# Rounding the transposed rows on ScalarE instead of VectorE in an attention and mixture-of-experts block

## The chip, the cores and the metric

The kernel runs on one core of one Trainium2 chip. The metric is device time in microseconds (us) of one execution. Three timed runs of the kernel before gave 1981.57, 1982.76 and 1986.39 us; the median is 1982.76 us. A further execution was recorded by the hardware profiler and took 1988.57 us, of which the trace covers a span of 1986.8 us.

The engines are named as in the trace: PE is TensorE (PEld its weight loads), ACT is ScalarE, DVE is VectorE, POOL is GpSimd, SP is SyncE, which issues most of the transfers.

## The reference

The input is 4 batches of 2048 rows of 512 floats. One block computes, cut to what matters here:

```
h = layernorm(x) * (1 + ca) + sa
x = x + ga * attention(h)            # segments of 128 rows, plus a global term
h = layernorm(x) * (1 + cb) + sb
x = x + gb * experts(h)              # 16 experts, top 1, capacity 512, D=512, H=2048
```

`sa, ca, ga, sb, cb, gb` are rows of 512 numbers for each batch, computed from a condition vector. The attention has `softmax(Q K^T / sqrt(32))` over 128 rows of a segment, all 512 features at once. The router takes the largest of 16 logits of every row.

## The kernel before

**Precision.** PE multiplies in a reduced float32 form (`fp32r`). To keep float32 accuracy, each operand `a` is split into `a_hi` (rounded to that form) and `a_lo = a - a_hi`, and each product is made of three matmuls (`split3`, lines 322 to 324): hi*hi, hi*lo, lo*hi.

**Stage 1, attention and router, until about 730 us.** The 8192 rows are worked off in 16 groups of 512 rows; `iteration(i)` of every engine works on group `i` and, in a software pipeline, on parts of groups `i-1`, `i-2` and `i-3`, and at its end prepares group `i+1`. The order on each engine is written out by hand, and semaphores tie the engines together. The folded weights `m` (query times key) and `v` (value times output) are split once before the loop. For the normalised, transposed rows of group `i+1` the steps at the end of an iteration are:

- PE, `transpose_xn`, line 602: 16 transposes of `xa` into the four PSUM banks `big[0..3]`, one bank for each chunk `k` of 128 features.
- ACT, `modulate`, line 957: for each `k` one activation `bank * (1 + ca) + sa` into `ht[:, k, :]`, an SBUF tile of 128x512 float32; both `(1 + ca)` and `sa` are 128x1 operands.
- DVE, `split_rows`, lines 1219 and 1221: for each `k` a copy `ht -> ht_hi` that rounds to fp32r (a CAST in the trace), then, after a wait for that copy, `ht_lo = ht - ht_hi`, and the semaphore `ht_split`.
- PE, `g_tile(i+1, 0)`: 12 matmuls into `big[0]`; before each chunk `k` it waits for `ht_split` of that chunk. `g_tile(i+1, 1)` to `(i+1, 3)` use the same rows again. `ht` itself is read once more by the score product (line 774), `ht_hi` and `ht_lo` by the `u` product with `v`.

After `g_tile 0` and `g_tile 1` PE transposes the second-norm rows `h2` of group `i-2` (line 706), ACT rounds them to `h2t_hi` (line 1032) and DVE makes `h2t_lo` (line 1368) for the router logits. DVE then goes through a long list: the statistics of the next rows (1150), softmax remainders, ranks of the router, `h` and `xr` (1387, 1391) from the attention output, statistics again, `u_lo` (1409) and the query constants (1275). PE may reuse a bank for the transposes of `xa` only when `u_lo` has been taken from it.

Meanwhile POOL scales and shifts the second-norm rows of group `i-1` in SBUF: four pairs of a multiply (line 1621) and an add (line 1625), each 128x512. PE's line 706 of the next iteration waits for all of them (`h2_ready`).

**Stage 2, the experts, from about 760 us.** For each of 16 experts rows are gathered by indirect DMA, and two layers of `split3` products run over weights that are loaded and split on the way. None of the lines of the change is used in it.

Of the kernel before, what the change touches and what calls it, by code (L numbers as in the profile page):

```python
# [30 lines left out]
ACT = mybir.ActivationFunctionType  # L31
# [29 lines left out]
def build_block(nc, x, wq, bq, wk, bk, wv, bv, wo, bo, wg, bg, w1, b1, w2, b2, cond, wmod, out):  # L61
# [39 lines left out]
    def keep(name, shape, dt):  # L101

        t, end = at(name, shape, dt, cursor[0])
        cursor[0] = end + (-end) % 32
        return t
# [7 lines left out]
    def over(start, *tensors):  # L113

        made = []
        for name, shape, dt in tensors:
            t, start = at(name, shape, dt, start)
            made.append(t)
        return made
# [12 lines left out]
    mod_col = keep("mod_col", [P, 2, KC, NBATCH], F32)  # L132
# [37 lines left out]
    ht = over(r_ht, ("ht0", full, F32), ("ht1", full, F32))  # L170
    ht_hi, ht_lo = over(r_split, ("ht_hi", full, F32R), ("ht_lo", full, F32R))
# [69 lines left out]
    def sem(name):  # L241
        return stack.enter_context(nc.semaphore(name))
# [23 lines left out]
    xr_in = [sem(f"xr_in{i}") for i in range(2)]  # L266
    grows_in = [sem(f"grows_in{i}") for i in range(2)]
    ln1_step, ln1_ready, ln1_rstd, xn_done = (sem(k) for k in ("ln1_step", "ln1_ready", "ln1_rstd", "xn_done"))
    t1_full, ht_full, ht_hi_done, ht_split, qc_raw, qc_ready = (sem(k) for k in (
        "t1_full", "ht_full", "ht_hi_done", "ht_split", "qc_raw", "qc_ready"))  # L270
    gt_full, gt_done, u_full, u_hi_done, u_split = (sem(k) for k in (
        "gt_full", "gt_done", "u_full", "u_hi_done", "u_split"))
    s_full, mx_step, negb_ready, exp_done, prec_ready, prob_ready = (sem(k) for k in (
# [43 lines left out]
    def batch_of(g):  # L317
        return g.n // GPB
# [13 lines left out]
    def pro_bank(q):  # L332
        return banks[q % 8 if q < MODS[GA] else 4 + q % 4]
# [586 lines left out]
    def _(act):  # L920
# [31 lines left out]
        def modulate(g):  # L952

            for k in range(KC):
                act.wait_ge(t1_full, 4 * g.n + k + 1)
                act.wait_ge(pro_evac, MCOL + 1)
                act.activation(ht[g.par][:, k, :], big[k][:, :], ACT.Identity,
                               bias=mod_col[:, 0, k, bass.ds(batch_of(g), 1)],
                               scale=mod_col[:, 1, k, bass.ds(batch_of(g), 1)]).then_inc(ht_full, 1)

        def add_u(g, j):

            act.wait_ge(gt_full, 4 * g.n + j + 1)
            act.activation(gt[:, j, :], big[j][:, :], ACT.Identity, bias=u_col[:, j:j + 1]).then_inc(gt_done, 1)

        modulate(Group(0, 0))
        modulation_row(GA)
        act.wait_ge(pro_full, HGT + 1)
        for k in range(KC):
            for b in range(NBATCH):  # L970
                seg = slice(b * (NSEG // NBATCH), (b + 1) * (NSEG // NBATCH))
                ins = act.activation(hg_t[:, k, seg], pro_bank(HGT)[:, k * NSEG + seg.start:k * NSEG + seg.stop],
                                     ACT.Identity, bias=mod_col[:, 0, k, b:b + 1], scale=mod_col[:, 1, k, b:b + 1])
# [6 lines left out]
        for k in range(KC):  # L980
            ins = act.activation(gg_t[:, k, :], pro_bank(GGT)[:, k * NSEG:(k + 1) * NSEG], ACT.Identity,
                                 bias=u_col[:, k:k + 1])
# [16 lines left out]
        def iteration(i, cur, prev, prev2, nxt, prev3):  # L999
# [57 lines left out]
            if nxt:  # L1057
                modulate(i.plus(1))
# [67 lines left out]
    def _(dve):  # L1126
# [88 lines left out]
        def split_rows(g):  # L1215

            for k in range(KC):
                dve.wait_ge(ht_full, 4 * g.n + k + 1)
                dve.tensor_copy(ht_hi[:, k, :], ht[g.par][:, k, :]).then_inc(ht_hi_done, 1)  # L1219
                dve.wait_ge(ht_hi_done, 4 * g.n + k + 1)  # L1220
                dve.tensor_tensor(ht_lo[:, k, :], ht[g.par][:, k, :], ht_hi[:, k, :].bitcast(F32), ALU.subtract) \  # L1221
                    .then_inc(ht_split, 1)

        split_rows(Group(0, 0))

        dve.wait_ge(gsum_xn, 1)
# [117 lines left out]
        def iteration(i, cur, prev, prev2, nxt, prev3):  # L1344
# [66 lines left out]
            if nxt:  # L1411
                split_rows(i.plus(1))
# [308 lines left out]
```

## Time and profile before

| quantity | value |
|---|---|
| median of three runs | 1982.76 us |
| profiled execution | 1988.57 us, span of the trace 1986.8 us |
| PE busy | 1866.8 us (94%), 9137 matmuls |
| DVE busy | 1315.1 us (66%), 2006 instructions |
| ACT busy | 780.6 us (39%), 1257 instructions |
| POOL busy | 863.5 us (43%), 709 instructions |
| mean granted clock of PE | 0.972 of full speed |

The shares are averages over two stages. From 194.0 to 686.0 us, which is twelve iterations of stage 1, PE is busy for 454.0 us, DVE for 445.7 us, POOL for 258.8 us and ACT for 183.9 us of 492 us, so DVE, not much of a bound over the whole span, is nearly as full as PE there.

A busy time in the trace includes the time in which an instruction has started and cannot yet proceed, for example because a memory port is held by another engine. So one line can have several durations.

### The profile page before, as it was taken

Reading aid. Unit: us, or ns where it says so; the run is one execution under the profiler, and the core shown is the slowest. Engines: PE = TensorE matmul, PEld = TensorE weight load, DVE = VectorE, ACT = ScalarE, POOL = GpSimd, SP = SyncE. Lnnn points to the kernel's source line nnn. Section 1 sums busy time; section 2 is a strip of 40 time slices with the busy share of each in tenths; the row PEclk is TensorE's granted clock in tenths of the full one; section 3 lists DMA queues with packets and bytes.
Section 4 is the critical chain, followed back from the end, with each engine's and each line's share of the span. In section 5 each row is a group of like instructions: output and inputs, shape, how many; then the busy total and the mean of one; then the engine's idle time right before and its main releaser. Section 6 shows DMA issues by size and latency. Waiting matters only on the chain.

```text
span 1986.8 us, 28205 instructions
## 1 busy us (share of the span) xinstructions
PE 1866.8 (94%) x9137; PEld 1517.2 (76%) x9138; DVE 1315.1 (66%) x2006; ACT 780.6 (39%) x1257; POOL 863.5 (43%) x709
## 2 busy tenths in 40 slices
PE   8998999989998973999999999999899999999998
PEld 3476777767777752788888888888888888888886
DVE  4378899998999875445655555354756878454763
ACT  2333333333343421333443433334535655333541
POOL 2034455644555443134434334233655766342632
PEclk9999999999999985999999999999999999999999
DMA  7143222332224342344354434434554556434531
GB/s 259 32 144 134 86 86 85 124 130 85 85 86 154 100 149 68 103 170 151 121 182 141 163 133 135 161 116 162 190 174 143 202 178 220 139 131 166 190 110 64
DMA packets 137916, 270.77 MB, mean 136 GB/s; under 512 B 17634, under 2 KB 18222, under 8 KB 137863
## 3 DMA queue, kind: packets, MB, share of 16 engines
q1 hardware_dynamic: 115338, 221.27, 31.8%
q0 software_dynamic: 22528, 48.86, 7.5%
q8 instruction: 29, 0.48, 0.1%
q14 instruction: 21, 0.16, 0.0%
HBM read 237.71 MB, written 50.72 MB: 145 GB/s over the span
## 4 chain that ended last, share of the span: by engine, by line
PE 70%; DVE 20%; issue 6%; ACT 2%; POOL 1%; DMA 1%; DVEq 0%; POOLq 0%; ACTq 0%; SPq 0%
PE bank L322 21%; PE bank L323 21%; PE bank L324 21%; DVE stats L1150 3%; DVE ht_hi L1219 3%; DVE ht_lo L1221 2%; DVE prob L1275 2%; DVE h L1387 2%; DVE xr L1391 2%; DVE u_lo L1409 1%; DVE h2t_lo L1368 1%; PE bank L817 1%; PE bank L563 1%; PE bank L531 1%; PE bank L591 1%
## 5 line engine op out<-in xcount | busy, mean ns | idle before, releaser
L1448 DVE TENSOR_TENSOR h_lo<-h_f,h_hi 128x512 fp32r<-128x512 f32 x256 | 221.0, 884 | 368.2 <-ACT h_f L1088 368.1
L1087 ACT ACTIVATE h_hi<-bank,b_col 128x512 fp32r<-128x512 f32 x256 | 176.4, 689 | 601.7 <-PE bank L324 589.9
L322 PE MATMUL bank<-bt_hi,w_hi 128*128 128x512 f32 (+4 forms) x1024 | 361.4, 353 | 7.8 <-DVE w_lo L1419 5.6
L323 PE MATMUL bank<-bt_lo,w_hi 128*128 128x512 f32 (+4 forms) x1024 | 360.3, 352 | 0.0
L324 PE MATMUL bank<-bt_hi,w_lo 128*128 128x512 f32 (+4 forms) x1024 | 360.2, 352 | 0.0
L322 PE MATMUL bank<-w_hi,h_hi 128*128 128x512 f32 x832 | 327.3, 393 | 3.8 <-DVE h_lo L1448 2.6
L323 PE MATMUL bank<-w_lo,h_hi 128*128 128x512 f32 x832 | 325.4, 391 | 0.0
L324 PE MATMUL bank<-w_hi,h_lo 128*128 128x512 f32 x832 | 325.1, 391 | 0.0
L322 PEld LDWEIGHTS bank<-bt_hi,w_hi 128*128 128x128 f32 x1024 | 195.4, 191 | 33.2 <-issue 9.0
L323 PEld LDWEIGHTS bank<-bt_lo,w_hi 128*128 128x128 f32 x1024 | 195.2, 191 | 21.1
L324 PEld LDWEIGHTS bank<-bt_hi,w_lo 128*128 128x128 f32 x1024 | 195.1, 191 | 20.4
L1644 POOL DMA_INDIRECT gb_rows<-mod_rows,tok_g x64 | 78.0, 1219 | 279.2 <-DVE tok_g L1525 221.7
L322 PEld LDWEIGHTS bank<-w_hi,h_hi 128*128 128x128 f32 x832 | 157.0, 189 | 36.9 <-issue 5.6
L324 PEld LDWEIGHTS bank<-w_hi,h_lo 128*128 128x128 f32 x832 | 156.9, 189 | 33.1
L323 PEld LDWEIGHTS bank<-w_lo,h_hi 128*128 128x128 f32 x832 | 157.1, 189 | 31.1
L1440 DVE TENSOR_TENSOR w_lo<-raw,w_hi 128x2048 fp32r<-128x2048 f32 x64 | 151.6, 2369 | 40.4 <-ACT w_hi L1077 40.4
L1644 POOL DMA_INDIRECT xh<-h_rows,tok_h x64 | 89.3, 1396 | 201.6 <-DVE tok_h L1507 178.2
L1088 ACT ACTIVATE h_f<-bank,b_col 128x512 f32<-128x512 f32 x256 | 174.3, 681 | 0.0
L1568 POOL TENSOR_TENSOR per_tok<-per_tok,half_neg 128x4 f32<-128x4 f32 (+1 forms) x33 | 33.4, 1013 | 279.7 <-DVE per_tok L1157 279.7
L1419 DVE TENSOR_TENSOR w_lo<-raw,w_hi 128x2048 fp32r<-128x2048 f32 x64 | 151.5, 2368 | 2.2
L322 PE MATMUL bank<-ht_hi,m_hi 128*128 128x512 f32 x256 | 113.6, 444 | 33.6 <-DVE ht_lo L1221 31.0
L1670 POOL TENSOR_TENSOR yo<-yo,gb_rows 128x512 f32<-128x512 f32 x60 | 98.5, 1642 | 106.4 <-DVE yo L1469 105.0
(256 smaller groups left out, 3375.1 us busy)
## 6 DMA issues: line engine op xcount, KB each, us to landing
raw<-in_L_ffn_W_dram SPq DMA_DIRECT2D x128, 1024.0 KB, 5.5
xa<-in_L_attn_x_dram SPq DMA_DIRECT2D x16, 1024.0 KB, 5.4
xr<-in_L_attn_x_dram SPq DMA_DIRECT2D x16, 1024.0 KB, 8.0
out_dram<-xr SPq DMA_DIRECT2D x16, 1024.0 KB, 9.9
h_rows<-h SPq DMA_DIRECT2D x16, 1024.0 KB, 4.6
b_bc<-in_L_ffn_b_dram SPq DMA_DIRECT2D x16, 256.0 KB, 6.3
wm_b<-in_L_wmod_dram SPq DMA_DIRECT2D x2, 1024.0 KB, 8.3
wm_d<-in_L_wmod_dram SPq DMA_DIRECT2D x2, 1024.0 KB, 5.1
```

What stands on the lines that cost most here:

```text
L322: pe.matmul(o, a_hi, b_hi, start=start, stop=False)
L323: pe.matmul(o, a_hi, b_lo, start=False, stop=False)
L324: return pe.matmul(o, a_lo, b_hi, start=False, stop=stop)
L1087: act.activation(h1_hi[b % 2][:, j, :], h_bank[j][:, :], ACT.Relu, bias=bias)
L1088: act.activation(h1_f[:, j, :], h_bank[j][:, :], ACT.Relu, bias=bias).then_inc(relu_done, 1)
L1150: dve.bn_stats(st[0:parts, s, :], rows[:, s, :]).then_inc(step, 1)
L1219: dve.tensor_copy(ht_hi[:, k, :], ht[g.par][:, k, :]).then_inc(ht_hi_done, 1)
L1419: dve.tensor_tensor(w1_lo[b % 2][:], raw[2 * (b % 2)][:], w1_hi[b % 2][:].bitcast(F32), ALU.subtract) \
L1440: dve.tensor_tensor(w2_lo[b % 2][:], raw[2 * (b % 2) + 1][:], w2_hi[b % 2][:].bitcast(F32), ALU.subtract) \
L1448: dve.tensor_tensor(h1_lo[b % 2][:, j, :], h1_f[:, j, :], h1_hi[b % 2][:, j, :].bitcast(F32), ALU.subtract) \
L1644: pool.indirect_dma_start(out=rows[:, j, :], out_offset=None, in_=source, in_offset=bass.IndirectOffsetOnAxis(tokens[:, j:j + 1], 0), boun ...
L1670: pool.tensor_tensor(yo[:, j, :], yo[:, j, :], gb_rows[:, j, :], ALU.mult).then_inc(y_scaled, 1)
```

## The change

ACT writes the rounded half itself. For each chunk it runs the same activation from the same PSUM bank twice, first into `ht_hi` (fp32r), then into `ht` (float32), and the semaphore `ht_full` is raised by the second. DVE's copy, and its wait for that copy, are gone; DVE only subtracts. The other splits of the kernel stay as they are.

```diff
-                act.activation(ht[g.par][:, k, :], big[k][:, :], ACT.Identity,
-                               bias=mod_col[:, 0, k, bass.ds(batch_of(g), 1)],
-                               scale=mod_col[:, 1, k, bass.ds(batch_of(g), 1)]).then_inc(ht_full, 1)
+                for rows in (ht_hi, ht[g.par]):
+                    ins = act.activation(rows[:, k, :], big[k][:, :], ACT.Identity,
+                                         bias=mod_col[:, 0, k, bass.ds(batch_of(g), 1)],
+                                         scale=mod_col[:, 1, k, bass.ds(batch_of(g), 1)])
+                ins.then_inc(ht_full, 1)
...
             for k in range(KC):
                 dve.wait_ge(ht_full, 4 * g.n + k + 1)
-                dve.tensor_copy(ht_hi[:, k, :], ht[g.par][:, k, :]).then_inc(ht_hi_done, 1)
-                dve.wait_ge(ht_hi_done, 4 * g.n + k + 1)
                 dve.tensor_tensor(ht_lo[:, k, :], ht[g.par][:, k, :], ht_hi[:, k, :].bitcast(F32), ALU.subtract) \
                     .then_inc(ht_split, 1)
```

On ACT, the end of the iteration of group 2 before (`logit_parts` are the router's partial logits, `ht_102` the rows of group 3, `prob` the softmax of the next iteration):

```order
L1014 ACTIVATE h_1_111<-xr_106,per_tok 128x512 x3
L1007 ACTIVATE u_hi<-bank 128x512
L1014 ACTIVATE h_1_111<-xr_106,per_tok 128x512
L1011 ACTIVATE logit_parts<-bank 32x512
L957 ACTIVATE ht_102<-bank,mod_col 128x512 x4
L1020 ACTIVATE prob,per_tok<-bank,per_tok 128x128 x4
```

and the same place in the changed kernel:

```order
L1016 ACTIVATE h_1_111<-xr_106,per_tok 128x512 x3
L1009 ACTIVATE u_hi<-bank 128x512
L1016 ACTIVATE h_1_111<-xr_106,per_tok 128x512
L1013 ACTIVATE logit_parts<-bank 32x512
L958 ACTIVATE ht_hi<-bank,mod_col 128x512
L958 ACTIVATE ht_102<-bank,mod_col 128x512
L958 ACTIVATE ht_hi<-bank,mod_col 128x512
L958 ACTIVATE ht_102<-bank,mod_col 128x512
L958 ACTIVATE ht_hi<-bank,mod_col 128x512
L958 ACTIVATE ht_102<-bank,mod_col 128x512
L958 ACTIVATE ht_hi<-bank,mod_col 128x512
L958 ACTIVATE ht_102<-bank,mod_col 128x512
```

Four activations have become eight; what stands before them and behind them is the same.

On DVE, the end of an iteration before (`ht_101` are the next group's rows):

```order
L1275 SCALAR_TENSOR_TENSOR prob,per_tok<-xa_100,vc_tab 128x512 x4
L1279 TENSOR_SCALAR per_tok<-per_tok,qc_bc 128x4
L1409 TENSOR_TENSOR u_lo<-bank,u_hi 128x512 x2
L1219 CAST ht_hi<-ht_101 128x512
L1221 TENSOR_TENSOR ht_lo<-ht_101,ht_hi 128x512
L1219 CAST ht_hi<-ht_101 128x512
L1221 TENSOR_TENSOR ht_lo<-ht_101,ht_hi 128x512
```

and the same place in the changed kernel:

```order
L1275 SCALAR_TENSOR_TENSOR prob,per_tok<-xa_100,vc_tab 128x512 x4
L1279 TENSOR_SCALAR per_tok<-per_tok,qc_bc 128x4
L1409 TENSOR_TENSOR u_lo<-bank,u_hi 128x512 x2
L1221 TENSOR_TENSOR ht_lo<-ht_101,ht_hi 128x512 x4
L1350 TENSOR_REDUCE per_tok<-bank 128x4
```

The pair of CAST and subtraction, which stood there four times, is one subtraction four times. PE, POOL and SP have the same rows as before.

## Rows read from the trace of the kernel before

**Rows 1.** Part 4 of the page: shares of the chain that ended last.

```profile
PE 70%; DVE 20%; issue 6%; ACT 2%; POOL 1%; DMA 1%; DVEq 0%; POOLq 0%; ACTq 0%; SPq 0%
```

**Rows 2.** Waits from 100 to 740 us: who waited for whom, us, times, longest.

```profile
PE bank L322 <- DVE ht_lo L1221: 31.0, 15, 2.2
...
PE bank L602 <- DVE u_lo L1409: 9.0, 12, 1.0
```

**Rows 3.** Timeline of PE, 437 to 446 us: start, duration, instruction, idle before.

```profile
437.86 0.39 PE L323 MATMUL bank<-ht_lo,m_hi 128*128 128x512 f32 x1
438.09 0.40 PE L324 MATMUL bank<-ht_hi,m_lo 128*128 128x512 f32 x1
440.57 0.50 PE L322 MATMUL bank<-ht_hi,m_hi 128*128 128x512 f32 x1 [2.08 <-DVE ht_lo L1221]
...
441.63 0.51 PE L322 MATMUL bank<-ht_hi,m_hi 128*128 128x512 f32 x1
441.98 0.39 PE L323 MATMUL bank<-ht_lo,m_hi 128*128 128x512 f32 x1
...
445.15 1.91 PE L706 MATMUL bank<-ident,h 128*128 128x128 f32 x16
```

**Rows 4.** Timeline of DVE, 432 to 449 us.

```profile
432.17 0.41 DVE L1219 CAST ht_hi<-ht 128x512 fp32r<-128x512 f32 x1
432.61 1.64 DVE L1221 TENSOR_TENSOR ht_lo<-ht,ht_hi 128x512 fp32r<-128x512 f32 x1
434.18 1.49 DVE L1219 CAST ht_hi<-ht 128x512 fp32r<-128x512 f32 x1
...
437.30 1.51 DVE L1219 CAST ht_hi<-ht 128x512 fp32r<-128x512 f32 x1
438.84 1.67 DVE L1221 TENSOR_TENSOR ht_lo<-ht,ht_hi 128x512 fp32r<-128x512 f32 x1
440.44 0.41 DVE L1219 CAST ht_hi<-ht 128x512 fp32r<-128x512 f32 x1
440.88 0.69 DVE L1221 TENSOR_TENSOR ht_lo<-ht,ht_hi 128x512 fp32r<-128x512 f32 x1
...
446.56 2.48 DVE L1368 TENSOR_TENSOR h2t_lo<-bank,h2t_hi 128x512 fp32r<-128x512 f32 x4 [1.50 <-ACT h2t_hi L1032]
```

**Rows 5.** Timeline of POOL, 430 to 440 us.

```profile
430.99 1.27 POOL L1621 TENSOR_TENSOR h<-h,cb_tab 128x512 f32<-128x512 f32 x1
432.44 1.27 POOL L1625 TENSOR_TENSOR h<-h,sb_tab 128x512 f32<-128x512 f32 x1 [0.18 <-POOL h L1621]
433.67 1.71 POOL L1621 TENSOR_TENSOR h<-h,cb_tab 128x512 f32<-128x512 f32 x1
435.56 1.27 POOL L1625 TENSOR_TENSOR h<-h,sb_tab 128x512 f32<-128x512 f32 x1 [0.18 <-POOL h L1621]
...
438.71 1.26 POOL L1625 TENSOR_TENSOR h<-h,sb_tab 128x512 f32<-128x512 f32 x1 [0.18 <-POOL h L1621]
```

**Rows 6.** Timeline of ACT, 430 to 434 us.

```profile
430.65 1.45 ACT L957 ACTIVATE ht<-bank,mod_col 128x512 f32<-128x512 f32 x2
```

**Rows 7.** Part 5 of the page, and lines by form: activations into either type.

```profile
L1087 ACT ACTIVATE h_hi<-bank,b_col 128x512 fp32r<-128x512 f32 x256 | 176.4, 689 | 601.7 <-PE bank L324 589.9
...
L957 ACT ACTIVATE ht<-bank,mod_col 128x512 f32<-128x512 f32 x64 | 46.1, 772 | 7.5 <-PE bank L602 7.0
```

**Rows 8.** Windows: length, busy PE, PEld, DVE, ACT, POOL, granted clock, DMA, GB/s.

```profile
153.00:194.00 41.00, 37.98 (x193) 29.94 (x193) 32.38 (x61) 15.04 (x30) 18.46 (x17) 0.96 0.30 103
...
440.60:480.40 39.80, 36.87 (x198) 28.98 (x198) 36.71 (x81) 15.43 (x31) 21.47 (x20) 1.00 0.30 105
...
482.00:484.00 2.00, 2.00 (x6) 1.59 (x5) 1.75 (x9) 1.60 (x10) 0.00 (x0) 0.50 0.85 324
...
644.40:686.00 41.60, 38.40 (x197) 30.03 (x197) 37.08 (x81) 15.19 (x31) 21.69 (x20) 0.96 0.24 81
```

**Rows 9.** Timeline of DVE at 116 us, in the first iteration.

```profile
116.36 0.69 DVE L1350 TENSOR_REDUCE per_tok<-bank 128x4 f32<-128x512 f32 x1 [1.02 <-PE bank L774]
```

More of the change, by code:

```diff
@@ L268, in build_block @@
     ln1_step, ln1_ready, ln1_rstd, xn_done = (sem(k) for k in ("ln1_step", "ln1_ready", "ln1_rstd", "xn_done"))
-    t1_full, ht_full, ht_hi_done, ht_split, qc_raw, qc_ready = (sem(k) for k in (
-        "t1_full", "ht_full", "ht_hi_done", "ht_split", "qc_raw", "qc_ready"))
+    t1_full, ht_full, ht_split, qc_raw, qc_ready = (sem(k) for k in (
+        "t1_full", "ht_full", "ht_split", "qc_raw", "qc_ready"))
     gt_full, gt_done, u_full, u_hi_done, u_split = (sem(k) for k in (
```

## The prediction

> **What bounds the kernel now.** I read the chain that ended last first: PE is most of it, but DVE has a fifth [rows 1], which is about 400 us, and DVE's lines in it (ht_hi, ht_lo, stats, h, xr, u_lo) belong to stage 1. So stage 1 is bound by PE and DVE in turn, and the list of waits says where they hand over: PE stood still 15 times, 31.0 us in all, for ht_lo, which comes from the routine that is changed, and 9.0 us in 12 waits of at most 1.0 us for u_lo [rows 2]. The next view is one steady iteration in time. PE has the first two chunks of g_tile 0 and then stops until 440.57, idle for 2.08 us; chunk 3 follows late at 441.63 [rows 3]. DVE at that time is inside split_rows, from 432.17 to 441.57, without a gap [rows 4].
>
> Why this takes 9.4 us for eight instructions is the thing to see. A CAST takes 0.41 us alone and 1.49 to 1.51 us in the middle, a subtraction 0.69 us alone and 1.64 to 1.67 us in the middle [rows 4]. The long ones end just after an instruction of POOL: POOL's add of 432.44 ends at 433.71 and DVE's subtraction at 434.25; POOL's multiply of 433.67 ends at 435.38 and DVE's CAST at 435.67 [rows 4, 5]. And that multiply takes 1.71 us instead of 1.27. The two engines take turns: whichever comes second stands until the other's instruction is through. When POOL is done, at 439.97, DVE is back at 0.41 and 0.69 us. The Trainium skill (SBUF — State Buffer, section "Who interferes with whom") says that VectorE copies, and subtractions with two SBUF inputs, share a port pair with GpSimd under an exclusive lock; the trace agrees with its 1.64 us against 0.69 us.
>
> The last view is the granted clock by windows of one iteration each. Of thirteen windows from 153 to 686 us, eight read 0.96 and five 1.00; the first, one at 1.00 and the last stand in [rows 8]. In each of the eight the clock is at its lower level, 1.2 GHz, only for a short stretch right behind the stall, as in the 2 us from 482 us, which read 0.50 [rows 8]; nowhere else in these iterations did it fall. A ninth such stretch follows the last stall, at 686 us.
>
> **The change part by part.** There are 16 calls of split_rows; one is in the prologue, one in the first iteration, and the other 14 are the crossings between iterations that show this stall.
>
> ACT, added: four more activations a group. Two of the old kind take 1.45 us back to back, so 0.725 us each [rows 6]. An activation that writes fp32r is not slower than one that writes float32 as far as rows show (0.689 us for h_hi with one column operand, 0.772 us for ht with two [rows 7]); bounds 0.689 and 0.772 us, less some overlap, I take 0.725. ACT begins at 430.65 [rows 6]; the pairs end at 432.1, 433.6, 435.0 and 436.5. Before, the first was there at 431.4. Nothing else is queued on ACT until the exponentials, which wait for DVE's maximum after 441.5; 2.9 us of more work lie in an idle stretch.
>
> DVE, removed: four CASTs, 0.41 + 1.49 + 1.51 + 0.41 = 3.8 us of its time, with what they waited for POOL in them. What is left is four subtractions which still meet POOL. I lay them out by the turns just read: after POOL ends, DVE is through in 0.54 us (433.71 to 434.25), and POOL's next one has started 0.13 us before that [rows 4, 5]. DVE is free at 432.17 and the first pair of ACT is there at 432.1; POOL's multiply ends at 432.26 and its add can only start at 432.44, so the first subtraction fits in front of it and ends near 432.9. Add 432.7 to 434.0; second subtraction to 434.5; multiply to 435.7; third (rows there at 435.0) to 436.2; add to 437.3; fourth (rows there at 436.5) to 437.9. So ht_lo is complete near 437.9 instead of 441.6, 3.7 us earlier.
>
> PE, the gain: chunk 2 would be wanted at 438.09 + 0.23 = 438.32 and chunk 3 at 439.0. Both subtractions are done by then, with 1.1 us to spare at chunk 3. Matmuls follow each other at 0.23 us (437.86 to 438.09). The stops cost 440.57 - 438.32 = 2.25 us; the three matmuls of chunk 2 then last until 441.63, 1.06 us instead of 0.69, since chunk 3 is late too; and the first step of chunk 3 is 0.35 us instead of 0.23 [rows 3]. Together 2.7 us a crossing, 0.6 of it above the idle time of 2.08. Over all: 31.0 us of idle time [rows 2] and 14 crossings of a little over 0.5 us, 7 us; 38 us.
>
> The clock: a window at 0.96 of 41.5 us has lost 0.04 * 41.5 = 1.7 us. Nine of these make 15 us. I expect them to go with the stall, because they only stand behind it, while the shorter stops for u_lo have none behind them. Bounds: 0 and 15 us; I take 15, by the row at 0.50 that lies behind a stop.
>
> What is late next: DVE's h2t_lo follows PE's line 706 by 1.41 us (446.56 after 445.15, DVE idle 1.50 before) [rows 3, 4]. PE reaches 706 2.7 us earlier, DVE is ready for it 3.7 us earlier, so DVE's idle time there grows to about 2.5 us and it stays tied to PE. From h2t_lo to u_lo DVE's list is unchanged, and it sets PE's wait for u_lo at line 602, 9.0 us over 12 iterations [rows 2], as before. That wait remains, since both of its ends move along with line 706. So the iteration becomes its old length less the stall: 39.8 - 2.7 = 37.1 us where the clock had held.
>
> POOL: its eight instructions end near 440.4 instead of 439.97, since the first subtraction now goes in front of an add. PE's line 706 of the next iteration, which waits for them, comes at 442.4 instead of 445.15. The cover shrinks from 5.2 us to 2.0 us; it holds. SP's transfers follow the same events and none of PE's waits in [rows 2] is for one, so I cost them at nothing.
>
> Where the change costs: in the first iteration POOL is not there, and CAST and subtraction took DVE 0.41 and 0.69 us as in the last pair of [rows 4], faster than ACT's pair of 1.45. Over four chunks that is 4 * (1.45 - 1.10) = 1.4 us later, but DVE idled 1.02 us there for PE's scores anyway [rows 9]; 0.5 us. The prologue is covered by PE's other products. I book 1 us for both, and 1 us for stops of PE at chunk 3 that I do not see.
>
> Sum: 38 + 15 - 2 = 51 us. The profiled execution took 1988.57 us (span 1986.8), so 1937.6 us by it. That execution stands 5.8 us above the median of the runs, 1982.76; against the median the forecast is 1932 us. Stage 2 is unchanged.
>
> **Rivals.**
>
> The clock keeps falling. Its low stretches may come from the thin work before the stall (transposes, the small score matmuls) and not from the stall itself. For it: five of the stalls of the same 2.08 us had no low stretch behind them, so the stall alone does not decide. Against it: all nine sit behind a stall, none elsewhere in the steady part. Then only the 38 - 2 = 36 us are gained: 1947 us.
>
> DVE loses a turn. If a subtraction arrives just after POOL has started, it stands for the whole of POOL's instruction. The first one has 0.2 us of margin at 432.26 to 432.44; if it misses, everything behind it moves by a turn of 1.67 us, the fourth ends near 439.6 and PE stops 0.7 us at chunk 3. If two are missed, PE stops 1.5 us or more; with 1.2 us won in a crossing and half of the clock it is 14 * 1.2 + 7 = 24 us, 1959 us. Of the skill's page the sentence "Issue order, not op shape, decides who blocks" says the same: who comes first decides; by it the order above holds only while ACT's pairs come in time.
>
> Slower: ACT's pair becomes the pace. If the activation into fp32r from this form cost so much that eight of them last beyond 441.6 - 0.7 - 430.65 = 10.2 us, that is above 1.28 us each, ht_lo would be later than now. At 1.4 us each PE would stop 1 us longer in each of 14 crossings: 1983 + 14 = 1997 us. The rows have nothing above 0.772 us for an activation of this size [rows 7], so this is remote.
>
> No gain: DVE's list is the true bound, and PE's lead is given back at line 602 as a longer wait for u_lo. Then 1981 us. Against it: DVE is idle 1.5 us before h2t_lo in the steady iteration, so DVE isn't what closes the loop, and it gets more idle there.
>
> **How the numbers follow.** Forecast 0.70, its own range 1924 to 1941. Clock stays 0.12 (1947). A turn or two lost 0.12 (1940 to 1962). No gain 0.03, slower 0.03. The range for 8 in 10 reaches from 1924, where the waits for u_lo also shrink by some 8 us, to 1956. A difference below 0.3%, 6 us, can't be told from none. Faster 0.94, same 0.03, slower 0.03.
>
> **What would show it.** In the profile after: the wait of line 322 for ht_lo gone or below 0.7 us in the steady iterations; the subtraction still at 1.1 to 1.7 us for most of them, so the port is still shared; ACT's pair at 1.45 us; DVE's idle time before h2t_lo up from 1.5 to about 2.5 us; the granted clock at 1.00 in the iteration windows; the iteration at 37 to 38 us; nothing moved behind 760 us but the start. The prediction is wrong if line 322 still waits 2 us, if line 706 waits for POOL, or if the wait at line 602 grows by what was saved.

## The result, and the profile after

Four runs of the changed kernel gave 1928.79 to 1933.73 us, median 1930.35 us; before it was 1984.58 us with one more run taken beside them. The ratio is 0.9727, 95% interval 0.9702 to 0.9752: 54 us faster, where 51 were forecast and 1932 us predicted. In a second set of runs the ratio was 0.9714 (0.9701 to 0.9727). The span of the trace went from 1986.8 to 1927.1 us, 59.7 us less; the profiled execution of the kernel before took 4 us more than its median, so the traces differ by more than the medians. Stage 2 (first matmul of the experts to the end) lasts 1198.9 us before and 1196.1 after, so all but 2.8 us of the 59.7 come in stage 1. One of the eight runs of the kernel before that stand beside the last two experiments took 6274.66 us; it is left out of their ratios.

The waits from 100 to 720 us in the changed kernel, as who waited for whom, us in total, times, longest; they answer to [rows 2]:

```profile
DVE ht_lo L1221 <- ACT ht L958: 19.3, 33, 2.3
...
PE bank L602 <- DVE u_lo L1409: 8.5, 12, 0.9
...
PE bank L322 <- DVE ht_lo L1221: 1.0, 2, 0.7
```

PE's 31.0 us in 15 waits for ht_lo are 1.0 us in 2, both at chunk 3, in the first two crossings (at 148.51 and 185.16 us). Its wait for u_lo stayed (9.0, now 8.5). The wait that is new is DVE's for ACT: the subtraction is bound by ACT's pace in places, and but for that 1.0 us PE comes later still and loses nothing by it.

PE from 406 us, one steady iteration, to be read against [rows 3] (start, duration, instruction):

```profile
406.03 0.48 PE L322 MATMUL bank<-ht_hi,m_hi 128*128 128x512 f32 x1
...
407.27 0.39 PE L324 MATMUL bank<-ht_hi,m_lo 128*128 128x512 f32 x1
407.50 0.39 PE L322 MATMUL bank<-ht_hi,m_hi 128*128 128x512 f32 x1
...
408.18 0.39 PE L322 MATMUL bank<-ht_hi,m_hi 128*128 128x512 f32 x1
...
411.58 1.91 PE L706 MATMUL bank<-ident,h 128*128 128x128 f32 x16
```

All 24 matmuls of g_tile 0 and 1 follow each other at about 0.23 us. From the first of them to line 706 it is 5.55 us; before it was 445.15 - 436.84 = 8.31 us, 2.76 more.

DVE in the same iteration, against [rows 4]; `x2` are two instructions in one row:

```profile
401.40 0.69 DVE L1221 TENSOR_TENSOR ht_lo<-ht,ht_hi 128x512 fp32r<-128x512 f32 x1
402.74 1.03 DVE L1221 TENSOR_TENSOR ht_lo<-ht,ht_hi 128x512 fp32r<-128x512 f32 x1 [0.64 <-ACT ht L958]
404.08 3.05 DVE L1221 TENSOR_TENSOR ht_lo<-ht,ht_hi 128x512 fp32r<-128x512 f32 x2 [0.31 <-ACT ht L958]
407.05 0.68 DVE L1350 TENSOR_REDUCE per_tok<-bank 128x4 f32<-128x512 f32 x1
407.77 0.53 DVE L1353 SCALAR_TENSOR_TENSOR per_tok<-per_tok 128x4 f32<-128x4 f32 x1
...
412.99 2.48 DVE L1368 TENSOR_TENSOR h2t_lo<-bank,h2t_hi 128x512 fp32r<-128x512 f32 x4 [1.56 <-ACT h2t_hi L1034]
```

The first subtraction is alone (0.69 us), the others take turns with POOL. From the first one's start to the last one's end it is 5.7 us, before with the CASTs 9.4 us.

ACT there, against [rows 6]:

```profile
399.92 0.78 ACT L958 ACTIVATE ht_hi<-bank,mod_col 128x512 fp32r<-128x512 f32 x1
400.60 0.77 ACT L958 ACTIVATE ht<-bank,mod_col 128x512 f32<-128x512 f32 x1
401.26 0.78 ACT L958 ACTIVATE ht_hi<-bank,mod_col 128x512 fp32r<-128x512 f32 x1
...
404.58 0.81 ACT L958 ACTIVATE ht<-bank,mod_col 128x512 f32<-128x512 f32 x1
```

And POOL, against [rows 5]:

```profile
400.18 1.27 POOL L1621 TENSOR_TENSOR h<-h,cb_tab 128x512 f32<-128x512 f32 x1
401.63 1.59 POOL L1625 TENSOR_TENSOR h<-h,sb_tab 128x512 f32<-128x512 f32 x1 [0.18 <-POOL h L1621]
...
406.54 1.74 POOL L1621 TENSOR_TENSOR h<-h,cb_tab 128x512 f32<-128x512 f32 x1
408.46 1.30 POOL L1625 TENSOR_TENSOR h<-h,sb_tab 128x512 f32<-128x512 f32 x1 [0.18 <-POOL h L1621]
```

ACT's pair comes every 1.33 us. POOL's add of 401.63 is longer (1.59 instead of 1.27): the first subtraction went in front of it. POOL ends at 409.76, 1.8 us before line 706 asks for its rows.

The granted clock in windows of 37 us, one that holds the crossing whose stall was the first with a low clock behind it before, and a later one (columns as in [rows 8]):

```profile
148.00:185.00 37.00, 36.12 (x192) 28.83 (x192) 29.23 (x56) 17.71 (x34) 20.28 (x18) 1.00 0.36 127
...
371.00:408.00 37.00, 36.12 (x198) 29.00 (x197) 32.98 (x77) 17.89 (x35) 21.95 (x21) 1.00 0.34 112
```

Every window from 111 to 631 us reads 1.00. An iteration lasts 37.15 us (line 602 at 215.05 and, eleven iterations later, at 623.68), where it had been 41.0 us on average (stalls at 193.98 and, twelve later, at 686.03). Fourteen crossings at 3.85 us are 54 us.

### The profile page after: what moved, and what is told of

It reads as the page before. It is cut to its first block, busy times and chain, and to the rows that moved or that the text cites. A ratio compares the mean times of both kernels' runs of the same rounds, so it can differ in the third digit from the quotient of the medians.

```text
span 1927.1 us, 28205 instructions
## 1 busy us (share of the span) xinstructions
PE 1839.8 (95%) x9137; PEld 1504.4 (78%) x9138; DVE 1258.2 (65%) x1942; ACT 822.6 (43%) x1321; POOL 871.1 (45%) x709
## 4 chain that ended last, share of the span: by engine, by line
PE 75%; DVE 16%; issue 5%; ACT 2%; POOL 1%; DMA 1%; DVEq 0%; POOLq 0%; ACTq 0%; SPq 0%
PE bank L322 22%; PE bank L324 22%; PE bank L323 22%; DVE stats L1152 3%; PE bank L774 3%; DVE prob L1275 2%; DVE h L1387 2%; DVE xr L1391 2%; DVE h2t_lo L1368 1%; PE bank L817 1%; PE bank L563 1%; DVE u_lo L1409 1%; PE bank L602 1%; PE bank L531 1%; PE bank L591 1%
## 5 line engine op out<-in xcount | busy, mean ns | idle before, releaser
L1079 ACT ACTIVATE w_hi<-raw 128x2048 fp32r<-128x2048 f32 x64 | 122.6, 1916 | 0.0
```

The source lines that it names most:

```text
L1079: act.activation(w2_hi[b % 2][:], raw[2 * (b % 2) + 1][:], ACT.Copy).then_inc(w2_hi_done, 1)
```

## The experiments

All are compared with the kernel before on the same chip. First, is it GpSimd that makes the CAST dear? Two kernels cut POOL's multiply and add of the second-norm rows to 4 of 512 columns, one of the kernel before and one of the changed kernel.

```diff
-                    rows = h2[p1.par][:, s, :]
+                    rows = h2[p1.par][:, s, 0:4]
...
-                    pool.tensor_tensor(rows, rows, cb_tab[:, bass.ds(b, 1), :].rearrange("p b d -> p (b d)"), ALU.mult) \
+                    pool.tensor_tensor(rows, rows, cb_tab[:, bass.ds(b, 1), 0:4].rearrange("p b d -> p (b d)"), ALU.mult) \
```

> The kernel before, but GpSimd's multiply and add of the second-norm rows (lines 1621 and 1625) touch only 4 of 512 columns, so the rows are left unscaled but for these. Theory A (VectorE's CAST and subtraction cost 3.8 us a group because they take turns with GpSimd): without these eight instructions the CAST takes 0.41 us and the subtraction 0.69 us every time, split_rows takes 4.4 us instead of 9.4, TensorE's stall for ht_lo and the low clock behind it go, and the time falls from 1984 to 1920 to 1932 us without any change of split_rows. Rival B (the time of the CAST is its own, GpSimd's overlap is a coincidence): CAST stays at 1.5 us in the middle pairs, the stall stays at 2.1 us, time 1980 to 1988 us.

Measured: 1912.59 us, ratio 0.9636 (0.9622 to 0.9651). Lines by form, 194 to 660 us, columns as in [rows 7]:

```profile
L1221 DVE TENSOR_TENSOR ht_lo<-ht,ht_hi 128x512 fp32r<-128x512 f32 x48 | 33.2, 692 | 1.6
L1219 DVE CAST ht_hi<-ht 128x512 fp32r<-128x512 f32 x48 | 20.2, 421 | 13.4 <-ACT ht L957 13.4
```

> The changed kernel with the same cut of GpSimd's multiply and add to 4 columns. Theory A: with no turns to take, the removed CAST is worth nothing more; the time equals that of the kernel before with the same cut, within 4 us, near 1920 us (0.8 us a group less than the changed kernel, since the query constants lose their turn too and u_lo is no longer late). Rival B: the gain of the change is independent of GpSimd, so this kernel is still some 50 us faster than the kernel before with the same cut.

Measured: 1910.73 us, ratio 0.9628 (0.9613 to 0.9643).

Rival B fell in both. With POOL's overlap gone the CAST takes 0.421 us and the subtraction 0.692 us each time, PE has no wait for ht_lo left, and the change is then worth 2 us instead of 54, which the intervals can't tell from none. Both times missed what I expected: the first is 7 us below the range, the second 9 us below 1920. Seen from line 706 to line 706 an iteration lasts 36.05 us in the second kernel, 1.1 us less than in the changed one where I had counted 0.8, and the last two, in which the loop runs out, are 3.3 and 0.8 us shorter; PE's wait of 3.1 us for POOL's last add is gone there. From its first expert matmul on, the first kernel takes the same 1196.1 us as the changed one, so none of the miss is in stage 2.

Second, each side of the change alone. ScalarE does its pair, and VectorE still copies:

```diff
+                for rows in (ht_hi, ht[g.par]):
+                    ins = act.activation(rows[:, k, :], big[k][:, :], ACT.Identity,
...
                 dve.tensor_copy(ht_hi[:, k, :], ht[g.par][:, k, :]).then_inc(ht_hi_done, 1)
```

> One part alone: ScalarE writes both halves as in the change, and VectorE still does its CAST into ht_hi. Theory A: ScalarE's four more activations lie in its idle time and the first chunk is ready no later than VectorE is; the same as before within 3 us (1982 to 1988). Rival C (the added work costs, and is hidden under a larger gain of the removal): 5 to 15 us slower than before, with TensorE's stall for ht_lo at 2.5 us or more.

Measured: 1983.35 us, ratio 0.9996 (0.9986 to 1.0007). With the CASTs in place the added work costs nothing that can be measured, so the gain comes with their removal. PE's wait, 100 to 720 us, is that of [rows 2] again:

```profile
PE bank L322 <- DVE ht_lo L1223: 31.7, 16, 2.2
```

Third, the clock. The stall is kept, and PE is given something to do in it:

```diff
             for k in range(KC):
+                if k == 2:
+                    for _ in range(filler):
+                        pe.matmul(lg_bank[:, :], m_hi[:, 0, chunk(0)], v_hi[:, 0, :], start=True, stop=True)
...
-                g_tile(i, 0)
+                g_tile(i, 0, 8 if prev2 else 0)
```

> The kernel before with eight more matmuls of 512 columns (0.23 us each, 1.8 us, into a bank that nothing reads then) in g_tile 0 ahead of chunk 2, that is inside the 2.1 us stall. Theory A (the low clock comes of the stall): the stall is still there in time, but TensorE is busy in it, the granted clock stays at 1.00 in the iteration windows, and the time falls by the clock's share of the forecast, some 15 us, to 1965 to 1973 us. Rival D (the low clock comes of the thin work around it): the clock still reads 0.96 in about eight windows and the time stays at 1984 us.

Measured: 1971.33 us, ratio 0.9933 (0.9918 to 0.9948), that is 13 us less for 8 more matmuls an iteration. The window from 194 to 640 us of this kernel, columns as in [rows 8]:

```profile
194.00:640.00 446.00, 430.17 (x2281) 337.69 (x2281) 410.56 (x883) 171.52 (x347) 237.61 (x220) 1.00 0.31 106
```

The same window of the kernel before:

```profile
194.00:640.00 446.00, 413.25 (x2154) 323.60 (x2155) 404.24 (x878) 168.66 (x341) 233.47 (x218) 0.98 0.29 100
```

Rival D fell: the transposes and the small products around the stall are the same, and the clock holds once PE is busy in it. Behind the eight matmuls PE still waits, 0.3 us in a steady crossing, so they don't make it later.

Fourth, how much room ScalarE has. The added activations go, inside the loop, to tiles that VectorE overwrites:

```diff
-                for rows in (ht_hi, ht[g.par]):
+                for rows in (*extra, ht_hi, ht[g.par]):
...
-                modulate(i.plus(1))
+                modulate(i.plus(1), (ht_lo,))
```

and in the second kernel `(ht_lo, h2t_lo)`.

> The changed kernel with a third activation for each chunk inside the loop, into ht_lo, where VectorE overwrites it. Each chunk then comes every 2.0 us (3 * 0.665) instead of 1.33. Theory A: rows of chunk 3 are ready 2.65 us later than in the changed kernel, at 7.98 + 0.1 us after ScalarE's start; TensorE wants the last ht_lo 8.3 us after that start, so it is late by 0.5 to 1.5 us with the turns: 0.5 to 1.5 us an iteration, 7 to 20 us slower than the changed kernel (1937 to 1951), and the clock stays high since the stall is short. Rival F (ScalarE's pair has room for a third activation): within 3 us of the changed kernel.

Measured: 1945.89 us, ratio 0.9801 (0.9786 to 0.9816); 17 us slower than the changed kernel beside it (1928.53), in the upper part of what theory A gave. Rival F fell.

> The changed kernel with four activations for each chunk, the added ones into ht_lo and h2t_lo, which VectorE overwrites. Chunks come every 2.66 us, the last after 10.6 us, ht_lo 11.4 us or more after ScalarE's start, when TensorE wants it at 8.3: theory A gives 3 us or more an iteration, 42 to 50 us, plus a low clock behind each longer stall (up to 25 us more where every iteration has one): 1975 to 2005 us, at or above the kernel before. This is the slower rival of the prediction put to the test, at 4 * 0.665 = 2.66 us a chunk. Rival F: TensorE's other waits absorb part of it, 1945 to 1970 us.

Measured: 2003.86 us, ratio 1.0096 (1.0079 to 1.0112), slower than the kernel before and at the upper end of theory A. PE's wait from 194 to 640 us with three activations:

```profile
PE bank L322 <- DVE ht_lo L1221: 6.8, 13, 0.7
```

and with four:

```profile
PE bank L322 <- DVE ht_lo L1221: 30.5, 21, 2.1
```

The windows over the same stretch read a clock of 1.00 with three and 0.96 with four: the stops of 0.5 to 0.7 us have no low stretch behind them there, while with four activations (stops of 1.9 to 2.2 us, most with a second one of 0.7 to 1.1 us close by) ten of the 14 crossings do. In its first iteration the kernel with three has one too, behind a stop of 0.68 and one of 1.04 us (0.50 from 120 to 122 us). The slower rival is a real mechanism: ScalarE's pace begins to cost between two and three activations a chunk, and between three and four the kernel falls behind the kernel before.

Last, the wait that is left, for u_lo. VectorE's list is reordered: one segment of the query constants stands before u_lo of bank 2, two before bank 3 and one behind it, where all four had stood before bank 2. The changed kernel runs beside it as reference.

> The changed kernel itself beside the others of this set, as their reference on the same chip: 1928 to 1934 us, ratio 0.972 to 0.975 to the kernel before. A gain that depends on the chip would show as a ratio outside of this.

Measured: 1928.53 us, ratio 0.9714 (0.9701 to 0.9727), a little below the 0.972 that I expected at least; the interval covers it. The edit of the next kernel:

```diff
-                    if s == 2:
-                        query_const(i)
+                    if s >= 2:
+                        query_const(i, (0,) if s == 2 else (1, 2))
                     dve.wait_ge(u_hi_done, 4 * n + s + 1)
...
+                query_const(i, (3,))
```

> The changed kernel with VectorE's order at the end of an iteration changed: the query constants (line 1275) of segment 0 stand before u_lo of bank 2, those of segments 1 and 2 before u_lo of bank 3, that of segment 3 and the closing line 1279 behind it, so that bank 3 is free about 1.7 us sooner. Theory A (TensorE's remaining wait at line 602, 0.63 to 0.89 us in most iterations, is VectorE's list being late with u_lo): the wait goes and 6 to 9 us with it, 1921 to 1925 us. Rival E (the wait is given back at once as a stall for ht_lo, since the subtractions start later against TensorE): a new stall of up to 0.8 us, time within 2 us of the changed kernel.

Measured: 1923.56 us, ratio 0.9688 (0.9675 to 0.9702), 5.0 us better than the changed kernel beside it (theory A had 6 to 9) and the fastest kernel here that leaves nothing out; the intervals of the two ratios touch, but the runs themselves do not overlap (1920.95 to 1925.25 against 1927.39 to 1929.11). Both theories had a part: the 8.5 us for u_lo are gone but for 0.3, and some came back as a wait for ht_lo (100 to 720 us):

```profile
PE bank L322 <- DVE ht_lo L1221: 4.9, 12, 0.7
```

I read this as the turns again: the query constants of line 1275 have both inputs in SBUF, and now two of the four meet POOL instead of one (1.83 and 1.16 us in the iteration at 394 us), so they take 1.07 us on average instead of 0.93.

I then moved the last segment behind split_rows:

```diff
-                query_const(i, (3,))
             if nxt:
                 split_rows(i.plus(1))
+            if cur:
+                query_const(i, (3,))
```

> As the reordered query constants on top of the change, but the last segment and the closing line 1279 stand behind split_rows. VectorE is then free for the subtractions some 2 us sooner and does the last segment in the 1.5 us that it idles before h2t_lo. Theory A: the 4.9 us that came back as waits for ht_lo go as well, 1917 to 1921 us. Rival G: the last segment, now between split_rows and the maximum of the scores, delays the exponentials and h2t_lo by about 1 us, which TensorE then waits for: 1923 to 1930 us.

Measured: 1957.54 us, ratio 0.9858 (0.9841 to 0.9874): theory A fell, and rival G had named the right place but far too small a price. Waits from 194 to 640 us:

```profile
PE bank L706 <- ACT gt L966: 15.2, 12, 1.6
DVE h2t_lo L1369 <- ACT h2t_hi L1034: 10.3, 12, 0.9
PE bank L322 <- DVE h2t_lo L1369: 5.3, 12, 0.4
```

The chain goes over three engines. The segment and line 1279 meet POOL and last 2.8 us; the maximum, and ACT's exponentials that wait for it, start later; and ACT's emptying of `gt` stands in its queue behind the exponentials, so PE can't reuse banks 0 and 1 for line 706. I had looked at DVE's idle time before h2t_lo and not at what ACT has queued behind the exponentials. Nor were the subtractions sooner by 2 us: DVE now waits 1.80 us for ACT before the first of them (at 415.91 us). And the clock fell again. Of the ten stops of 1.1 to 1.6 us for `gt`, each followed by one of 0.4 to 0.6 us for h2t_lo, six have a low stretch behind them; the four stops of 0.6 to 0.7 us have none. One of the six:

```profile
427.83 1.24 PE L706 MATMUL bank<-ident,h 128*128 128x128 f32 x8 [1.50 <-ACT gt L966]
429.62 0.66 PE L322 MATMUL bank<-ht_hi,m_hi 128*128 128x512 f32 x1 [0.44 <-DVE h2t_lo L1369]
...
430.00:432.00 2.00, 2.00 (x6) 1.56 (x5) 2.00 (x5) 0.30 (x1) 0.00 (x0) 0.50 0.94 318
```

> The kernel before with the query constants reordered as in the first of these kernels and nothing else. Theory A (in the kernel before, the last thing that PE waits for in an iteration is ht_lo, and that is set by VectorE's own list, not by when PE gets bank 3): the wait for u_lo at line 602 goes, the stall for ht_lo grows by as much, and the time stays within 4 us of the kernel before. Rival H (waits of PE add up, each can be taken away on its own): 5 to 9 us faster, as it was on top of the change.

Measured: 2001.65 us, ratio 1.0088 (1.0073 to 1.0103), 17 us slower. Both theories missed it. PE's stalls in one iteration:

```profile
400.65 0.51 PE L322 MATMUL bank<-ht_hi,m_hi 128*128 128x512 f32 x1 [1.25 <-DVE ht_lo L1221]
...
403.77 0.79 PE L322 MATMUL bank<-ht_hi,m_hi 128*128 128x512 f32 x1 [2.15 <-DVE ht_lo L1221]
```

The window from 194 to 640 us:

```profile
194.00:640.00 446.00, 409.48 (x2068) 322.05 (x2080) 396.15 (x854) 159.77 (x330) 228.12 (x210) 0.94 0.28 99
```

Theory A had the direction: the wait at line 602 is gone and the wait for ht_lo took its place. But it is larger than the one it replaced (3.4 us against 2.1 + 0.8). Two of the query segments now meet POOL instead of one, and DVE's list from its first u_lo to the first CAST lasts 7.7 us instead of 7.3. The clock is lower for it (0.94 against 0.98), with a low stretch in every crossing. Rival H fell. The same edit gains 5 us on one kernel and costs 17 us on the other; I read that as what the change did: in the kernel before DVE's list decides when an iteration ends, in the changed one it no longer does.

## Why the prediction was right

- **What bounds the kernel.** Right. The turns with POOL make the price of the CAST (the cut of POOL's work took it away), and the stall for ht_lo is where most of it reaches PE. The waits for u_lo (9.0 us) went with POOL's work as well, so they hang on the turns too.
- **ScalarE's pair costs nothing.** Right, by the kernel that has only this part: 0.9996. I had 1.45 us for a pair; it is 1.33 us, since the step between activations back to back is 0.66 to 0.67 us and I had spread the whole time of two.
- **The turns of the four subtractions.** Right: 5.7 us laid out, 5.7 us in the trace. The one margin that I had called thin, the first subtraction in POOL's gap, held in each iteration from 215 us on (0.68 or 0.69 us). In the second crossing it took 1.15 us, and there PE stopped for 0.28 us.
- **The stall.** 38 us forecast, somewhat too low. The filler kernel splits the gain: 13 us belong to the clock, so 41 us are left for the stall and what hangs on it. What I had not booked is a second stop. I took 39.8 us as the length of an iteration in which the clock holds, but some such iterations last 40.6 or 40.7 us, with a stop of 0.4 us for line 1387 (`h`) in the middle and a later u_lo:

```profile
416.95 0.50 PE L322 MATMUL bank<-v_hi,ht_hi 128*128 128x512 f32 x1 [0.40 <-DVE h L1387]
```

  PE has five of these (1.9 us; some 0.9 us each with what follows, so about 4 us, an estimate) in the kernel before. The kernels that still have the CASTs all have five, with POOL's work cut too; the kernels without the CASTs have none. Why the change takes them away stays open.
- **The clock.** 15 us forecast, 13 us by the filler kernel, and all windows of the loop at 1.00 after. The nine low stretches were those of the one execution that was profiled, 1988.57 us, 4 us above the median. The kernel with only ScalarE's pair, which has the same stall, shows six, and took 1980.97 us; so 15 us was near by some luck, and the share of the clock differs between executions.
- **What is late next.** Half right. h2t_lo follows line 706 by 1.41 us as before, and the waits for u_lo stayed. But DVE's idle time there is 1.56 us and not 2.5: POOL now ends later against DVE's list, so small instructions behind split_rows meet it (line 1353, 0.53 us instead of 0.16; line 1297, 0.67 instead of 0.22). 0.8 of the 0.9 us went into these two. Nothing hung on it.
- **Where it costs.** The 1 us booked for stops at chunk 3 came: 1.0 us in two waits, in the first crossings. The 1 us for the first iteration and the prologue was not needed; PE has no wait for ht_lo there. The first iteration has a difference between the traces that is not the change's. Its 16 transposes took 3.59 us at a low clock before and 1.97 after:

```profile
109.12 3.59 PE L602 MATMUL bank<-ident,xa 128*128 128x128 f32 x16 [1.96 <-POOL xa L1578]
```

  They take 1.96 or 1.97 us in all ten other kernels' traces too, the filler kernel's and that with only ScalarE's pair among them, and in the changed kernel's second trace. So the 1.6 us belong to that one execution of the kernel before. The idle 1.02 us of DVE [rows 9], on which I counted, came of the same low clock.
- **The sum.** 51 us against 54 of the medians. Between the two traces, to which its terms belong, it is 59.7 us: besides what was booked, some 4 us of the stops for `h`, 1.6 us of the transposes and 2.8 us of stage 2. The first is the part of the change that I missed. The other two belong to the execution: stage 2, 1198.9 us in the trace before, lasts 1194.9 to 1197.3 us in the eleven others, with the CASTs and without.
- **The rivals.** The clock rival fell to the filler kernel. A lost turn was not seen in the steady iterations. The slower rival, put at 1.28 us or more for an activation, was brought about with four activations a chunk, that is 1.33 us for each of the old two, and gave 2004 us, more than the 1997 us that I had for 1.4 us: I had left out that the stops make the clock fall.

## What to carry to other kernels

Where two engines take turns, the price of an instruction is what it waits for, not what it computes: the CAST of 0.42 us cost 1.5 us in the middle, twice a group. Moving it to ScalarE, whose activation takes 0.78 us with POOL's work and with that work cut, was worth 54 us, and the second activation cost nothing. Before you take an engine's idle time for room, follow what its neighbours have queued behind the event you delay; 1.5 us of idle time in DVE was not room for one segment. And a wait that is not the last in its iteration can't be taken away alone: the same reordering gained 5 us after the change and lost 17 before it.

## What was not expected of the hardware

The stall of 2.1 us in each crossing cost PE some 13 us through the clock, beside the 41 us of the stall and what hung on it; eight useless matmuls in it made the kernel 13 us faster. Not every stall had a low stretch behind it: nine of 14 in the kernel before, six of 14 with ScalarE's pair added. Shorter stops could have one as well, six of the ten of 1.1 to 1.6 us with a shorter one close behind; single stops of 0.4 to 1.0 us in the loop had none. What decides in a given crossing stays open.
